# Two transposed row blocks of a decoder layer: from TensorE to DMA, with the loads issued by ScalarE

## What is computed

```
x = layernorm(x + self_attention(x))               # causal, 16 heads of 32
x = layernorm(x + cross_attention(x, context))     # 77 context rows
logits = x_norm @ c_norm.T + x @ w_route.T         # 8 experts
gates  = softmax over the two highest logits
x = layernorm(x + sum_e gates[e] * (gelu(x @ w1[e] + b1[e]) @ w2[e] + b2[e]))
```

## Time and profile before

| | |
|---|---|
| median of 3 runs | 2484.53 us (2479.5 to 2484.94) |
| the profiled execution | 2485.55 us, its span 2483.2 us |
| TensorE busy | 2365.9 us, 95% of the span |
| VectorE, ScalarE, GpSimd busy | 64%, 48%, 44% |
| second half (chunk chains and experts) | from about 1364 us to the end |
| one chunk in it, from output product to output product | 140.9 us |

### The profile page before, as it was taken

One profiled execution on the slowest core, in us unless ns is written; L12 is line 12 of the kernel. 1 busy time (PEld: TensorE's weight loads), 2 busy tenths in 40 slices (PEclk: granted clock), 3 DMA queues, 4 the chain that ended last, 5 costly groups with the idle time before them and its releaser, 6 DMA issues. The chain is left out here.

```text
span 2483.2 us, 36648 instructions
## 1 busy us (share of the span) xinstructions
PE 2365.9 (95%) x13612; PEld 999.0 (40%) x13612; DVE 1598.2 (64%) x3854; ACT 1182.0 (48%) x2197; POOL 1090.2 (44%) x441
## 2 busy tenths in 40 slices
PE   7999799999999999999996799999999999999998
PEld 3444222323232323233333354554455454544443
DVE  4443397777777777777724466757566675757564
ACT  4332156666666666666654242443435343434431
POOL 0000259999999999999932112020212112021100
PEclk9999799999999999999998899999999999999999
DMA  7874502131313121223100401010010101010000
GB/s 245 288 246 161 132 6 74 32 74 32 74 32 74 32 74 36 70 70 73 32 14 14 183 1 65 1 48 18 16 50 1 65 1 48 18 48 18 1 18 17
DMA packets 130478, 155.05 MB, mean 62 GB/s; under 512 B 19854, under 2 KB 98190, under 8 KB 129277
## 3 DMA queue, kind: packets, MB, share of 16 engines
q1 hardware_dynamic: 130301, 152.72, 20.1%
HBM read 99.99 MB, written 52.17 MB: 61 GB/s over the span
## 5 line engine op out<-in xcount | busy, mean ns | idle before, releaser
L787 ACT ACTIVATE probs<-st_ps 128x512 f32<-128x512 f32 (+3 forms) x1280 | 611.6, 535 | 359.0 <-PE st_ps L901 201.3
L654 POOL TENSOR_TENSOR total<-total,probs 128x2048 f32<-128x2048 f32 (+3 forms) x190 | 667.7, 3514 | 45.6 <-ACT probs L787 26.1
L836 DVE TENSOR_REDUCE seg_max<-s_ps 128x1 f32<-128x512 f32 x768 | 505.9, 685 | 139.5 <-PE s_ps L887 137.4
L1553 PE MATMUL fps<-x2T,w_p_hi 128*128 128x512 f16 x1024 | 318.6, 379 | 0.0
L1553 PE MATMUL fps<-w_p_hi,hT 128*128 128x512 f16 x1024 | 304.8, 379 | 2.8 <-DVE x L1501 1.7
L840 DVE CUSTOM_DVE_ANT_0 s_ps<-s_ps,later 128x384 f32<-128x384 f32 (+3 forms) x512 | 248.8, 499 | 68.4 <-issue 68.3
L1300 ACT ACTIVATE hidden<-fps,keep_b_sb 128x512 f32<-128x512 f32 x128 | 87.7, 685 | 348.8 <-PE fps L1553 346.1
L1222 POOL TENSOR_TENSOR keep_soft<-keep_soft,ssum 128x1232 f32<-128x1232 f32 x32 | 71.6, 2250 | 401.6 <-DVE ssum L1392 401.6
L887 PE MATMUL s_ps<-keep_work,keep_soft 96*128 96x512 f16 (+3 forms) x640 | 219.8, 361 | 21.6 <-DMA keep_soft<-q_parts 11.6
L1505 DVE SCALAR_TENSOR_TENSOR x<-fps,gates_un,x 128x512 f32<-128x512 f32 x256 | 182.1, 742 | 87.5 <-PE fps L1553 85.3
L901 PE MATMUL st_ps<-keep_soft,keep_work 98*128 98x512 f16 (+3 forms) x640 | 220.7, 354 | 12.7 <-issue 5.4
(11 more groups left out here) (200 smaller groups left out, 3614.2 us busy)
## 6 DMA issues: line engine op xcount, KB each, us to landing
keep_soft<-xT_in SPq DMA_DIRECT2D x8, 1024.0 KB, 6.2
q_parts<-qk_out SPq DMA_DIRECT2D x32, 256.0 KB, 3.5
k_parts<-qk_out SPq DMA_DIRECT2D x32, 256.0 KB, 3.9
keep_work<-w_in SPq DMA_DIRECT2D x8, 1024.0 KB, 8.7
v_rows<-v_out SPq DMA_DIRECT2D x32, 256.0 KB, 2.1
w_parts<-piece_cut SPq DMA_DIRECT2D x8, 1024.0 KB, 5.6
inv<-inv_rows SPq DMA_DIRECT2D x32, 256.0 KB
o_parts<-o_out SPq DMA_DIRECT2D x32, 256.0 KB, 2.6
```

Source lines behind the costliest of these rows:

```text
L654: last = nc.gpsimd.tensor_tensor(summed[:, :, off:], other[:, :, off:], probs[:, k % NP, :, off:], ALU.add)
L787: nc.scalar.activation(probs[:, k % NP, h, off:], st_ps[:, p % (2 * NVU) % RING, off:], ACT.Exp, scale=SCALE).then_inc(exp_done.sem, 1)
L836: nc.vector.reduce_max(highest, s_ps[:, slot], AX.X).then_inc(s_read.sem, 1)
L1553: last = nc.tensor.matmul(bank, lhs(a, t), rhs(b, t), start=(n == 0), stop=(n == len(steps) - 1))
```

## The change

ScalarE now makes the upper part of a row block straight from the normalised rows in SBUF, VectorE the lower part beside it, both in row order, into `row_parts` (a part of `soft` that is free at that time). SyncE waits for each lower part and issues one transposing DMA per row block, from `row_parts` into `x1T` or `x2T`, four per turn. `query` and `route` wait for these DMAs. The transposes on TensorE and their eight PSUM banks per chunk go. The loads that SyncE issued, the weights and each chunk's `load_rows` and `load_context`, are issued by ScalarE: the weights before its first instruction of the second half, the others in the stage `norm2`. PLAN moves units: `norm1` 1 (was 3) and `turn1` 7 (5), `out2` 4 (6), `norm2` 2 (3), `turn2` 5 (2). In the tail of attention the stages from `query` on stand two steps later.

```
-    PLAN = [("out", 1), ("norm1", 3), ("turn1", 5), ("query", 1), ("scores0", 2), ("scores1", 7), ("scores2", 6),
+    PLAN = [("out", 1), ("norm1", 1), ("turn1", 7), ("query", 1), ("scores0", 2), ("scores1", 7), ("scores2", 6),
...
-            ("pv2", 3), ("pv3", 1), ("out2", 6), ("norm2", 3), ("turn2", 2), ("route", 4), ("gate", 0)]
+            ("pv2", 3), ("pv3", 1), ("out2", 4), ("norm2", 2), ("turn2", 5), ("route", 4), ("gate", 0)]
...
-        "sp": [(-40, 0)],
+        "sp": [(-40, "load"), (31, "turn")],
...
+    row_parts = soft[:].rearrange("p j h s -> p (j h s)")[:, TT * D:2 * TT * D].bitcast(F16).rearrange(
+        "p (j s n) -> p j s n", j=TT, s=2)
...
 # SyncE
+            def turn(i, u, which):
+                dst = x2T[parity(u)] if which else x1T
+                for j in range(TT):
+                    sp.wait_ge(lo_ready.sem, at(lo_ready, i, u, which * TT + j))
+                    sp.dma_start(dst[:, :, :, j * P:(j + 1) * P].rearrange("p s t n -> p (s t) n"),
+                                 row_parts[:, j].rearrange("p s n -> p (s n)"),
+                                 transpose=True).then_inc(turn_done, 16)
...
                     for u in range(2):
-                        load_next(i, u)
+                        turn(i, u, 0)
+                        turn(i, u, 1)
                         store(i, u)
...
 # ScalarE
                 if stage in ("turn1", "turn2"):
-                    k0, dst = (AT_T1, x1T) if stage == "turn1" else (AT_T2, x2T[p])
+                    src, done = (x1, 0) if stage == "turn1" else (x2[p], TT)
                     for j in parts:
-                        bank = wait_product(i, u, k0 + j)
-                        nc.scalar.activation(dst[:, 0, :, j * P:(j + 1) * P], bank.rearrange("p (t n) -> p t n", t=KT),
-                                             ACT.Copy, scale=XS).then_inc(hi_ready.sem, 1)
+                        act.wait_ge(normed.sem, at(normed, i, u, done + j))
+                        nc.scalar.activation(row_parts[:, j, 0], src[:, j], ACT.Copy,
+                                             scale=XS).then_inc(hi_ready.sem, 1)
+                elif stage == "norm2" and chunk(i, u) + 1 < NC:
+                    act.wait_ge(dve_read.sem, at(dve_read, i, u, nth(USES, AT_O + TT - 1)))
+                    load_rows(act, S, x_rows, o_parts, chunk(i, u) + 1)
+                    load_context(chunk(i, u) + 1)
...
             def rest():
+                for r in range(3):
+                    act.dma_start(b2_sb[r * GP:r * GP + E], b2).then_inc(b2_loaded, 16)
+                for dst, src in weights:
+                    act.dma_start(dst, src).then_inc(w_loaded, 16)
                 split_b2()
...
 # VectorE
+            def rows_lo(i, u, src, which, hi_index):
+                for j in range(TT):
+                    dve.wait_ge(hi_ready.sem, at(hi_ready, i, u, hi_index + j))
+                    nc.vector.scalar_tensor_tensor(row_parts[:, j, 1], src[:, j], XS, row_parts[:, j, 0], ALU.mult,
+                                                   ALU.subtract).then_inc(lo_ready.sem, 1)
...
 # TensorE
-                elif stage in ("turn1", "turn2"):
-                    k0, src, done = (AT_T1, x1, 0) if stage == "turn1" else (AT_T2, x2[p], TT)
-                    for j in parts:
-                        pe.wait_ge(normed.sem, at(normed, i, u, done + j))
-                        bank = chain_bank(i, u, k0 + j)
-                        for t in range(KT):
-                            cols = slice(t * P, (t + 1) * P)
-                            last = nc.tensor.transpose(bank[:, cols], src[:, j, cols], ident[:])
-                        last.then_inc(c_ready.sem, 1)
                 elif stage == "query":
-                    pe.wait_ge(dve_read.sem, at(dve_read, i, u, nth(USES, AT_T1 + TT - 1)))
+                    pe.wait_ge(turn_done, turned_at(chunk(i, u), 0))
...
                 elif stage == "route":
-                    pe.wait_ge(dve_read.sem, at(dve_read, i, u, nth(USES, AT_T2 + TT - 1)))
+                    pe.wait_ge(turn_done, turned_at(chunk(i, u), 1))
```

More of the change, by code:

```diff
@@ L737, in step @@
                 for piece in first_at("sp", s, end):
-                    sp.wait_ge(pv_done.sem, pv_done.at(i, NKU - 1))
+                    if piece == ["load"]:
+                        sp.wait_ge(pv_done.sem, pv_done.at(i, NKU - 1))
                     chain(*piece)
@@ L1000, in chains @@
     SCALE = DH ** -0.5
-    USES = (["dve"] * TT + ["dve"] * TT + ["act"] * KT + ["dve"] * (TT * NG)
-            + ["act"] * HG + (["act"] * HG + ["dve"]) * (NG - 1) + ["dve"] + ["dve"] * TT + ["dve"] * TT
+    USES = (["dve"] * TT + ["act"] * KT + ["dve"] * (TT * NG)
+            + ["act"] * HG + (["act"] * HG + ["dve"]) * (NG - 1) + ["dve"] + ["dve"] * TT
             + ["dve"])
-    AT_OUT, AT_T1, AT_Q = 0, TT, 2 * TT
+    AT_OUT, AT_Q = 0, TT
     AT_S = AT_Q + KT
@@ L1035, in chains @@
     VALUE = ("probs0", "probs1", "pv0", "probs2", "pv1", "probs3", "pv2", "pv3")
-    value_at = [(87 + n, stage) for n, stage in enumerate(VALUE)]
+    value_at = [(89 + n, stage) for n, stage in enumerate(VALUE)]
     first_chain = {
-        "sp": [(-40, 0)],
[L1039 to L1046, removed]
+        "sp": [(-40, "load"), (31, "turn")],
+        "pool": [(-100, "rows"), (12, "out"), (62, "scores1"), (68, "scores2"), (74, "scores3")] + value_at,
+        "act": [(24 + j, "turn1", j) for j in range(TT)] + [(39 + 3 * o, "query", o) for o in range(KT)]
+        + [(59, "scores0"), (65, "scores1"), (69, "scores2"), (73, "scores3")] + value_at,
+        "dve": [(-2, "out"), (14, "norm1"), (24, "turn1"), (52, "scores0"), (58, "scores1"), (64, "scores2"),
+                (68, "scores3")] + value_at,
+        "pe": [(4 * j - 2, "out", j) for j in range(TT)] + [(36 + 3 * o, "query", o) for o in range(KT)]
+        + [(52, "scores0"), (58, "scores1"), (64, "scores2"), (68, "scores3")] + value_at,
     }
@@ L1084, in chains @@
         hi_ready = count("hi_ready", TT + NG + TT)
+        lo_ready = count("lo_ready", 2 * TT)
+        turn_done = sem("turn_done")
         biased = count("biased", 2 * TT)
@@ L1176, in store, with first @@
                              x2[u][:]).then_inc(stored[u], 16)
+            def first(what):
+                if what == "load":
+                    load_context(0)
+                else:
+                    turn(-1, 1, 0)
             def rest():
                 start_stored(sp, stored)
[L1180 to L1184, removed]
+                turn(-1, 1, 1)
                 for i in range(LOOPED):
                     for u in range(2):
-                        load_next(i, u)
+                        turn(i, u, 0)
+                        turn(i, u, 1)
                         store(i, u)
+                turn(LOOPED, 0, 0)
+                turn(LOOPED, 0, 1)
                 store(LOOPED, 0)
@@ L1192, in rest @@
                     sp.wait_ge(s, stored_at(NC // 2))
-            return load_context, rest
+            return first, rest
         def pool_work(pool):
@@ L1249, in act_work @@
         def act_work(act):
+            load_context = context_loader(act)
             def begin():
@@ L1405, in chain @@
                 elif stage == "turn1":
-                    for j in range(TT):
-                        cols = slice(j * P, (j + 1) * P)
-                        lo_part(i, u, AT_T1 + j, j, x1T[:, 1, :, cols], x1T[:, 0, :, cols])
+                    rows_lo(i, u, x1, 0, 0)
                 elif stage.startswith("scores"):
@@ L1433, in chain @@
                 elif stage == "turn2":
-                    for j in range(TT):
-                        cols = slice(j * P, (j + 1) * P)
-                        lo_part(i, u, AT_T2 + j, TT + NG + j, x2T[p][:, 1, :, cols], x2T[p][:, 0, :, cols])
+                    rows_lo(i, u, x2[p], 1, TT + NG)
                 elif stage == "route":
```

24 lines of the change are left out of this document (11 added, 13 removed).

## The result

The changed kernel takes 2556.76 us (median of 4 runs, 2552.77 to 2557.3) against 2483.77 us before: 1.029 times as long, interval 1.0278 to 1.0304. Its profiled execution has a span of 2554.9 us, 71.7 more than before. The forecast was 2560 us.

A forecast was written before the change was run, and what follows sets the result against it. TensorE was taken to bound the second half. First turn 3.4, second turn 2.3 and clock 4.2 made 9.9 us per chunk, times seven 69.6, plus 5.4 for start and tail: +75, so 2560 us; range 2480 to 2680.

The forecast's parts named there:

- What bounds: Second half: TensorE, busy 140.40 of 141.00 us, sets the time; whatever leaves its queue is gained, every wait paid in full.
- First turn: Before the query product: four transposes land 8.2 us after the first lower part; wait 5.2 us, query 3.4 us later.
- the row of the 1 MB load in 1 KB pieces: Trace's 1 MB loads in 1 KB pieces land after 8.2 us; taken as the landing of a turn's four transposes.
- an issue that holds SyncE for longer than a landing: On SyncE: a DMA issue holding the queue longer than a landing would show the prediction wrong altogether.
- Second turn: Before the routing product: four transposes land 8.2 us after the first lower part; wait 4.1 us, routing 2.3 us later.
- GpSimd's contention: Second turn: GpSimd's four bias additions lie on VectorE's lower parts, each taking 1.43 us, not 0.69.
- Clock: TensorE behind both waits: two waits of 4 to 5 us lower the clock, costing 2.1 us each, 4.2 per chunk.
- Loads on ScalarE: Load issues moved from SyncE to ScalarE: cost nothing; 2.6 us a chunk lost if their cover were gone.
- Start and tail: First looped chunk 4.4 us later behind ScalarE's held issue, tail of attention +1 us; together 5.4 us.
- Sum: Whole kernel: 9.9 us per chunk times seven, 69.6, plus 5.4 for start and tail; +75 us, 2560 us.
- rival of slow pieces: Transposing DMAs: 256-byte pieces slow the landing, four take 20.2 us (2748 us) or 12 us (2621); chance 0.23.
- Plain copies: Each transpose lands 2.1 us behind its lower part, 2467 to 2488 us; chance 0.30 with what lies between, to 2515.

The follow-up runs named there:

- e6: The changed kernel with GpSimd's four bias additions for the next chunk made two stages later, in the gate stage; 2543.17 us, 1.0230 times before.
- e5: The changed kernel with all loads back on SyncE; 2560.58 us, 1.0306 times before.
- e9: The changed kernel with two transposing DMAs of 512 KB per turn in place of four of 256 KB; 2550.94 us, 1.0261 times before.
- e11: The changed kernel with the order of units as before the change; 2604.73 us, 1.0476 times before.

## Why the prediction was right

**What bounds.** Right: the waits of 4.3 and 4.6 us and the 3.7 us of lower clock, less the 3.5 us of transposes, make 9.1 of the 9.4 us that a chunk lost. So the waits put into TensorE's queue were paid nearly in full.

**First turn.** That TensorE would wait for the landing was right, what makes the landing late was not. From the end of the output product to the query it was 13.7 us before (1831.73 to 1845.45, the query's start in the earlier trace rows) and is 16.1 now (2015.3 to 2031.42): +2.4, where +3.4 was said. The term that was mis-sized is the landing: 7.2 us from the first lower part, not 8.2. I took the row of the 1 MB load in 1 KB pieces, as if the transfer set the time. The runs show a row of four issues of 1.33 us and 3.3 us for the last (3 x 1.34 + 3.2 = 7.2); that both come out alike is luck, as the 128 KB and 1 MB runs show (9.1 and 6.7 us behind the last lower part, for the same bytes). The prediction had named an issue that holds SyncE for longer than a landing as a sign of being wrong altogether. One issue doesn't (1.33 against 3.3 us), but the row of four does, with 5.4 us, and no term of the sum stood for it.

**Second turn.** The wait was 4.1 us in the prediction and is 4.34 in this chunk, 4.6 in the mean; routing +2.6 where +2.3 was said. GpSimd's contention is real (1.8 us a chunk by e6), but lies elsewhere: I let all four lower parts take 1.43 us under it; here hidden unit 14's and the first of the four were slowed, since the additions were 2.6 us old when hidden unit 14's lower part began. That unit's extra 1.0 us, which I had not counted, and the landing, counted 1 us too long, nearly cancel.

**Clock.** 4.2 us a chunk predicted; the query lost 1.86 and routing with its units 1.88 in the chunk shown, and keeping TensorE on returned 3.7.

**Loads on ScalarE.** Costed at nothing in a chunk, and e5 agrees within 0.2 us. The issues stand where hidden unit 14's gelu was not yet ready (timeline of ScalarE):

```profile
1977.56 0.39 ACTq L989 DMA_DIRECT2D keep_x<-x_rows_in  x1
...
1984.60 0.69 ACT L1325 ACTIVATE hidden<-fps,keep_b_sb 128x512 f32<-128x512 f32 x1 [6.42 <-PE fps L1583]
```

**Start and tail.** The held issue is there, 7.08 us on ScalarE's queue, and the landing that I put at 1399.8 came at 1400.5 (timeline of ScalarE, then of SyncE):

```profile
1381.00 7.08 ACTq L1164 DMA_DIRECT2D keep_kv<-k_blocks  x1
...
1388.95 2.19 ACT L1285 ACTIVATE keep_soft<-x 128x512 f16<-128x512 f32 x4 [12.76 <-issue]
...
1390.33 8.31 SPq L1183 DMA_TRANSPOSE x2T<-keep_soft  x4
```

That the landing agrees is luck as well: the first lower part was ready at 1390.3 and not 1391.6, and the four issues took 8.31 us there and not 5.4 (the second alone 4.26), with loads still under way.

The output product so begins at 1402.0, 5.4 us later than before where 4.4 was said; the tail lost nothing.

**Sum.** Said: 9.9 us a chunk and 5.4 beside. Found: 9.4 a chunk. In the span: 6.8 to the first query, 6 x 9.42 = 56.5 to the last, 8.4 behind it, 71.7. In the rival of slow pieces, only 16.4 of the 25 us for start and tail is worked out (4.4 and 12); nothing here hangs on the rest.

**Rivals.** Plain copies fell: they needed a landing within 2.7 us of the last lower part, and it was 5.4. The rule that stood beside it (the Trainium skill, Advanced Engine Details and Errata, X-Bar Transpose (TRN2): transposing transfers as fast as plain ones) is not decided by the landing of one transfer here: 3.3 us for 256 KB lies between plain stores of that size (2.1 to 3.9). What the runs add to it is the issue, 1.33 us against 0.32. Issued with the last lower part, and not 2.2 us behind it, the last DMA would have landed some 3.2 us after it (an estimate from the chain above), still past the 2.7 that the rival needed. Slow pieces fell as well: four land in 7.2 us, not in 12 to 20.

## What to carry to other kernels

Before work is taken off a bound engine, compare what leaves its queue (here 1.75 us) with the whole way that replaces it, from the last producer through the issues to the landing (here 5.4 us); unless the plan has that much other work to put there, the bound engine waits, and pays a second time at the lower clock. Count DMA issues as instructions of their queue: a row of them can set the landing more than the bytes do, and of the four sizes tried here 512 KB was best. And where an order of work is filled to the brim, time saved at one wait is partly taken back at the next, so price edits by the chunk, not by the wait.

## What the runs showed of the hardware that I had not expected

- A transposing DMA's issue held SyncE for 1.26 us (128 KB), 1.33 (256 KB), about 2.1 (512 KB) and 4.84 us (1 MB). The plain loads issued by ScalarE in the chunk shown took 0.36 to 0.67 us each.
- At the start of the second half, with loads still under way (350 to 400 GB/s), such an issue took 4.52 us (e5) and up to 5.46 us (e9).
- A DMA of 256 KB turns eight tiles of 128x128 (four of each part), so 1.33 us of issue is 0.17 us for a tile. The Trainium skill (VectorE: DVE Perf Modes, The three transpose paths) gives 1309 ns for one tile by DMA; that is close to the hold of one issue here, whatever it moved up to 256 KB, and not to the price of a tile.
- An expert-shaped VectorE instruction, 0.69 us alone, took 1.67 us beside GpSimd's additions, and four took 6.45 us (e11).
